# First maximum blocks between half pieces, first keys loaded a chunk sooner, a store wait moved, TensorE's loops written out

## What is computed

```
q = proj(Wq, bq) / math.sqrt(hd);  k = proj(Wk, bk);  v = proj(Wv, bv)
attn = softmax(einsum('bnd,bmd->bnm', q, k), axis=-1)
fuse = einsum('bnm,bmd->bnd', attn, v)
hybrid = conv1x1(concat([x, fuse]), Wf, bf);  x = hybrid * m + x * (1 - m)
# then: depthwise 3x3, gate, 1x1, depthwise 3x3, 1x1, times x
```

## Time and profile before

| what | value |
|---|---|
| median of 3 runs | 4018.02 us (4016.7 to 4024.36) |
| profiled execution, its own time | 4009.41 us |
| its span, first to last instruction | 4007.6 us |
| TensorE busy | 3786.8 us, 94% |
| projection ends, first exponential starts | 281.2 us |
| last exponential starts | 3531.6 us |

### The profile page before, as it was taken

The page is one execution under the profiler, slowest core; times in us unless marked ns, Lnnn a source line. Parts: engine busy times, 40 slices in busy tenths (PEclk is TensorE's granted clock), DMA queues, the critical chain, the costliest instruction groups (busy, mean ns, idle before and its releaser), DMA issues. The chain is left out here.

```text
span 4007.6 us, 74947 instructions
## 1 busy us (share of the span) xinstructions
PE 3786.8 (94%) x19317; PEld 2028.8 (51%) x19317; DVE 3046.2 (76%) x5030; ACT 2923.2 (73%) x5512; POOL 2958.6 (74%) x1359
## 2 busy tenths in 40 slices
PE   7879999999999999999999999999999999959797
PEld 4445555555555555555555555555555555424343
DVE  3357888877877877888777878887778887528989
ACT  1238888888878888888888888888888888812212
POOL 3337888888888888888888888888889888930000
PEclk9989999999999999999999999999999999979898
DMA  6942212221112112212221122112221111122121
GB/s 205 275 126 41 43 22 23 44 43 22 23 27 43 32 22 32 43 32 22 32 43 32 22 33 43 32 22 33 43 32 22 23 22 22 12 76 61 41 64 42
DMA packets 297551, 187.66 MB, mean 47 GB/s; under 512 B 199170, under 2 KB 223924, under 8 KB 297156
## 3 DMA queue, kind: packets, MB, share of 16 engines
q1 hardware_dynamic: 297348, 185.18, 23.8%
HBM read 123.28 MB, written 61.47 MB: 46 GB/s over the span
## 5 line engine op out<-in xcount | busy, mean ns | idle before, releaser
L848 DVE TENSOR_REDUCE block_max<-mx 128x1 f32<-128x512 f32 (+1 forms) x3584 | 2520.5, 759 | 661.0 <-PE mx L619 641.4
L763 ACT ACTIVATE prob<-st 128x512 f32<-128x512 f32 x4096 | 2109.7, 616 | 385.5 <-PE st L608 359.9
L394 POOL TENSOR_TENSOR prob_sum<-prob_sum,prob 128x1024 f32<-128x1024 f32 x768 | 1826.5, 2394 | 26.0 <-POOL prob_sum L394 17.0
L608 PE MATMUL st<-queries,keys 97*128 97x512 f32 x4096 | 1593.6, 409 | 60.6 <-ACT prob L763 36.2
L619 PE MATMUL mx<-keys,max_queries 96*128 96x512 f32 x4096 | 1566.4, 407 | 35.2 <-issue 18.4
L394 POOL TENSOR_TENSOR prob_sum<-prob 128x1024 f32<-128x1024 f32 x384 | 915.9, 2385 | 360.9 <-PE acc L651 345.4
L608 PEld LDWEIGHTS st<-queries,keys 97*128 97x128 f32 x4096 | 772.1, 190 | 539.1 <-issue 236.0
L619 PEld LDWEIGHTS mx<-keys,max_queries 96*128 96x128 f32 x4096 | 777.9, 190 | 431.1 <-ACT tail_exp L753 167.0
L631 PE MATMUL acc<-prob,values 128*32 128x512 f32 x8192 | 993.5, 603 | 0.0
L753 ACT ACTIVATE tail_exp<-mx,negated_max 128x1024 f32<-128x1024 f32 x512 | 575.2, 1123 | 115.5 <-DVE negated_max L852 83.4
L631 PEld LDWEIGHTS acc<-prob,values 128*32 128x32 f32 x8192 | 215.2, 109 | 495.1 <-ACT prob L763 283.0
(11 more groups left out here) (102 smaller groups left out, 1207.5 us busy)
## 6 DMA issues: line engine op xcount, KB each, us to landing
max_queries<-q_scratch SPq DMA_DIRECT2D x384, 64.0 KB
queries<-q_scratch SPq DMA_DIRECT2D x384, 64.0 KB
keys<-k_scratch SPq DMA_DIRECT2D x168, 128.0 KB, 4.8
q_scratch<-keys SPq DMA_DIRECT2D x64, 256.0 KB, 4.8
k_scratch<-keys SPq DMA_DIRECT2D x32, 512.0 KB, 5.1
prob<-in_x SPq DMA_DIRECT2D x16, 512.0 KB, 4.0
v_scratch<-prob SPq DMA_DIRECT2D x16, 512.0 KB, 5.3
queries<-negated_max SPq DMA_DIRECT2D x512, 0.5 KB, 2.0
```

The costliest lines, as they stand in the source:

```text
L394: nc.gpsimd.tensor_tensor(psum[k][:, :, :], a, prob[:, (first + i) % RING, :, :], ALU.add).then_inc(added, 1)
L608: nc.tensor.matmul(st[bank(i, p)][:, :], kk[gp][0:SPLIT + 1, h, s * P:(s + 1) * P], qq[p][:, h, :], start=True, stop=True).then_inc(scores, 1)
L763: nc.scalar.activation(prob[:, s % RING, h, :], st[bank(i, p)][:, :], ACT.Exp).then_inc(exp_done, 1)
L848: nc.vector.tensor_reduce(bmax[p][:, hn, k:k + 1], banks.rearrange("p b n -> p (b n)"), AX.X, ALU.max, negate=True).then_inc(mx_taken, 1)
```

## The change

Five things. `blocks_at` now gives out blocks behind each half of a piece: TensorE issues half a piece (one matmul of q or k, two of v), then one or two blocks. VectorE reduces the blocks of a piece's first half and only then takes the piece before (`take_piece`). SyncE loads the first keys, values and queries after the stores of chunk 8, not 9. ScalarE's wait for the last stores moves from ahead of unit 0 to its exponentials 16 and 28. TensorE's loops over units are written out, with constants in its waits. The sums and products are the same.

```diff
-def blocks_at(n, i):
+def blocks_at(n, i, half):
...
-    slots = BLOCK_CHUNKS * len(PIECES)
-    at = (n - PLAIN_CHUNKS) * len(PIECES) + i
+    slots = BLOCK_CHUNKS * len(PIECES) * 2
+    at = ((n - PLAIN_CHUNKS) * len(PIECES) + i) * 2 + half
     return range(FIRST_BLOCKS * at // slots, FIRST_BLOCKS * (at + 1) // slots)
...
-                if n == PLAIN_CHUNKS - 2:
+                if n == PLAIN_CHUNKS - 3:
...
-            def project(n, p, i):
+            def project(n, p, i, half):
...
-                    for kt in range(CT):
-                        mm = nc.tensor.matmul(pq[k % 2][:, :], w[:, kt, j * P:(j + 1) * P], x[p][:, kt, :],
-                                              start=(kt == 0), stop=(kt == CT - 1))
-                    mm.then_inc(qk_ready, 1)
+                    mm = nc.tensor.matmul(pq[k % 2][:, :], w[:, half, j * P:(j + 1) * P], x[p][:, half, :],
+                                          start=(half == 0), stop=(half == 1))
+                    if half == 1:
+                        mm.then_inc(qk_ready, 1)
...
-            with pe.Fori(0, PAIRS // 2 - 1) as g2:
-                pair(g2, 0, True)
-                pair(g2, 1, True)
-            pair(PAIRS // 2 - 1, 0, True)
-            pair(PAIRS // 2 - 1, 1, False)
+            for u in range(UNITS):
+                unit(u, u % 2, u // NCH % 2, keys_and_queries(u + 1), keys_and_queries(u + 2))
...
+                    if not prev and i == RING:
+                        act.wait_ge(low_ready, 4 * (STEPS + 2))
+                    if not prev and i == 2 * RING - 4:
+                        for q in range(2):
+                            act.wait_ge(v_stored[q], 16 * (1 + STEPS // 2))
...
-            act.wait_ge(low_ready, 4 * (STEPS + 2))
-            for p in range(2):
-                act.wait_ge(v_stored[p], 16 * (1 + STEPS // 2))
...
-                for i, piece in enumerate(PIECES):
-                    if piece[0] == "v":
-                        take_values(n, n % 2, int(piece[1]))
-                    else:
-                        split_projected(n, n % 2, 2 * "qk".index(piece[0]) + int(piece[1]))
-                    for j in blocks_at(n, i):
+                for i, half in itertools.product(range(len(PIECES)), range(2)):
+                    for j in blocks_at(n, i, half):
                         maxima(j // MAXMM, j // MAXMM, older=False, blocks=(j % MAXMM,))
+                    if half == 0 and n * len(PIECES) + i > 0:
+                        take_piece(n * len(PIECES) + i - 1)
+            take_piece(STEPS * len(PIECES) - 1)
```

More of the change, by code:

```diff
@@ L1 @@
+import itertools
 from contextlib import ExitStack
@@ L576, in _ @@
             pe.sem_inc(sums_done, SUMS)
-            def project(n, p, i):
+            def project(n, p, i, half):
                 piece, j = PIECES[i][0], int(PIECES[i][1])
-                if i == 0:
+                if i == 0 and half == 0:
                     pe.wait_ge(x_loaded[p], 16 * (n // 2) + 16)
                 if piece == "v":
-                    pe.wait_ge(v_copied, 2 * n + j + 1)
-                    for s in range(2):
-                        m = 2 * j + s
-                        for kt in range(CT):
[L588 to L593, removed]
+                    if half == 0:
+                        pe.wait_ge(v_copied, 2 * n + j + 1)
+                    m = 2 * j + half
+                    for kt in range(CT):
+                        mm = nc.tensor.matmul(pv[j][:, half, :], x[p][:, kt, m * P:(m + 1) * P], keep["wv"][:, kt, :],
+                                              start=(half == 0 and kt == 0), stop=(kt == CT - 1),
+                                              skip_group_check=True)
+                    if half == 1:
+                        mm.then_inc(v_ready, 1)
+                        if j == 1:
+                            pe.drain().then_inc(x_used, 1)
                 else:
@@ L596, in project @@
                     w = keep["wq" if piece == "q" else "wk"]
-                    pe.wait_ge(full_ready, 4 * n + k + 3)
-                    for kt in range(CT):
-                        mm = nc.tensor.matmul(pq[k % 2][:, :], w[:, kt, j * P:(j + 1) * P], x[p][:, kt, :],
-                                              start=(kt == 0), stop=(kt == CT - 1))
-                    mm.then_inc(qk_ready, 1)
+                    if half == 0:
+                        pe.wait_ge(full_ready, 4 * n + k + 3)
+                    mm = nc.tensor.matmul(pq[k % 2][:, :], w[:, half, j * P:(j + 1) * P], x[p][:, half, :],
+                                          start=(half == 0), stop=(half == 1))
+                    if half == 1:
+                        mm.then_inc(qk_ready, 1)
             def score(u, p, gp, i):
@@ L680, in unit, with keys_and_queries @@
                         max_block(u + 2, p, after[0], n - MAXMM)
[L682 to L693, removed]
+            def keys_and_queries(w):
+                if w >= UNITS:
+                    return None
+                g, c = divmod(w, NCH)
+                return g % 2, Q_INC * (w // 2 + 1), KV_INC * (g // 2 + 1) if c == 0 else None
             for n in range(STEPS):
-                for i in range(len(PIECES)):
-                    project(n, n % 2, i)
-                    for j in blocks_at(n, i):
+                for i, half in itertools.product(range(len(PIECES)), range(2)):
+                    project(n, n % 2, i, half)
+                    for j in blocks_at(n, i, half):
                         if j == 0:
@@ L788, in _ @@
                         take_projected(n, n % 2, 2 * "qk".index(piece[0]) + int(piece[1]))
-                    for j in blocks_at(n, i):
+                    for j in (*blocks_at(n, i, 0), *blocks_at(n, i, 1)):
                         if j % MB == MB - 1:
@@ L822, in take_values, with take_piece @@
                 ins.then_inc(v_copied, 1)
+            def take_piece(at):
+                n, i = divmod(at, len(PIECES))
+                piece, j = PIECES[i][0], int(PIECES[i][1])
+                if piece == "v":
+                    take_values(n, n % 2, j)
+                else:
+                    split_projected(n, n % 2, 2 * "qk".index(piece) + j)
             def invert(v):
```

## The result

The changed kernel took 3965.13 us in the median of six runs (3962.3 to 3982.95), the kernel before 4017.4 (4015.49 to 4024.36) beside it: 52 us less. The ratio over all runs is 0.9878 (95% interval 0.9855 to 0.99); that of the two medians would be 0.987. The forecast was 29.4 us less. The direction is right; the time lies 3.9 us under the low end of the range. The profiled execution's span fell by 47.1 us, from 4007.6 to 3960.5.

| stage | before | after | difference | forecast |
|---|---|---|---|---|
| TensorE goes on in chunk 11 | 167.92 | 167.81 | −0.1 | +1.7 |
| last maximum block starts | 268.9 | 254.8 | −14.1 | −4.5 |
| first exponential starts | 281.2 | 258.2 | −23.0 | −13.1 |
| first to last exponential | 3250.4 | 3225.7 | −24.7 | −16.3 |
| from there to the end | 476.0 | 476.7 | +0.7 | 0 |

What follows compares the result with a forecast made beforehand. TensorE, busy 94% of the span, was taken as the bound, so gains come from its waits or stage ends. Stages ahead 14.1 plus loops 15.3 gave 29.4 us: 4018.0 to 3988.6 us, range 3969 to 4005.

Steps and rivals of the forecast that it cites:

- First keys: At chunk 11, TensorE's 11.1 us wait for keys becomes 14.7 us for the input: 3.5 us lost, bounds 2 to 6.
- The estimate from the rate in the same page's specifications: Loads ahead of chunk 11's input: at 27 GiB/s per DMA engine, 4.6 MB pass in 10 us, input in time.
- Half pieces: Blocks ahead of attention: 5 us from shorter tail waits plus 3 us of clock, 8 us saved, bounds nothing to 12.
- half pieces save nothing: Rival, blocks ahead of attention: VectorE is full and the clock stays low, 8 us less gain; chance 0.18.
- ScalarE's wait: Before attention: first exponential starts once tail and score are there, at 268.1 not 281.19; the moved waits cost nothing.
- Loops written out: Attention: removed outer jumps 7.6 us, clock behind them 5, inner jumps 2.7; sum 15.3 us, bounds 8 and 20.
- The register work behind the waits costs nothing: Attention loops: a block follows a score in 0.23 us there too, so constants in waits were given no gain.
- the clock's 5 us behind outer jumps: Attention: granted clock 0.66 for 5 us and 0.72 for 12 after the outer jumps; 5 us to be won.
- The step on instruction pages: Attention: straight code fetches some 90 more instruction pages, costed at nothing.
- the rival of late pages: Attention: instruction pages held back by the busy DMA queue stop TensorE; at 0.5 us each 4033 us; chance 0.04.
- The likeliest case: Whole kernel: the forecast itself, 3980 to 3996 us; chance 0.55.
- constants in the waits speed up every unit: Rival, attention: half of 0.8 us idle per unit comes back over 60 units, 25 us, giving 3964; chance 0.08.

Runs made afterwards that it cites:

- input_first: The changed kernel with chunk 11's input issued ahead of the first keys; ratio 0.9909 to the kernel before.
- split_loads: input_first with only the first head's keys and six query rows loaded early, the rest behind chunk 10's stores; 3940.01 us, ratio 0.985 to the kernel before.
- halves_only: The kernel before with blocks behind half pieces and VectorE's new order; keys, ScalarE's wait and loops as before; ratio 0.9977.
- inner_out: The changed kernel with TensorE's outer loop back and inner loops written out, so units 1 to 47 wait on registers; 3988.89 us, ratio 0.9973 to the kernel before.
- outer_only: The kernel before with only TensorE's outer loop written out, inner loops and register waits kept; ratio 1.003.
- after_again: The changed kernel run again unchanged, on the chip of the third group; 3954.65 us, ratio 0.99 to the kernel before.
- loops_only: The kernel before with TensorE's loops over units written out and nothing else; ratio 0.9923.

## Why the prediction was right and wrong

**First keys: right, with the loss put 1.8 us too high.** The wait for keys became a wait for chunk 11's input, at the place and with the releaser forecast. The input took 18.3 us to land where 18.9 was assumed, but it was issued at 149.45 instead of 151, and TensorE was back at 167.81 instead of 169.6 (168.6 and 169.35 in two other profiles). With a piece less done that is a loss of 1.7 us where 3.5 was forecast, just under the lower bound of 2. input_first and split_loads show the cause to be the order of the queue: put ahead of the loads, the same input is in time. The Trainium skill's rule on the ring order (DMA: Bandwidth & Descriptors, section Queues, rings and completion order) agrees with this. The estimate from the rate in the same page's specifications does not: by it the input would have come in time, while the DMA engines moved 284 GB/s from 154.6 to 167.8 us with their share at 1.02.

**Half pieces: the mechanism right, the term mis-sized, 8 forecast and 15.8 measured** (14.1 us of the last block and 1.7 of the pause), over its upper bound of 12. Two terms were too small. The waits for the tail fell by 9.4 us, not 5: I had VectorE's start no better than 0.5 us after block 7, and left the pair 0.7 to 1.0 us of wait; the mean is 0.6. And the lost clock came back whole: the 10.2 us at the lower level in this stretch (three dips, two of them in the windows of the earlier trace rows) are gone, about 5.1 us of work, of which I had taken half without a row for it. At the start of the stretch, behind the pause, the clock was low for 3.2 us instead of 6.5, an estimated 1.6 us more. That is 16.1, against 15.8 measured. The rival "half pieces save nothing" is refuted by halves_only. (The forecast's 269.3 for the last block is TensorE's first score; the last block starts at 268.9.)

**ScalarE's wait: right.** From the last block to the first exponential it was 12.3 us before, 3.4 now, 8.9 saved, and 8.6 was forecast (269.3 to 281.2 against 264.8 to 268.1). No moved wait stops ScalarE. That it is also what lets half pieces count in full was not said: without it, halves_only lost 5 us.

**Loops written out: the step that failed is "The register work behind the waits costs nothing".** The term stood at 0 in a sum of 15.3 with 20 as its upper bound, and the attention gave 24.7. Of these the jumps explain 7.6 + 2.7, the low clock (46.8 us before, 41.0 after) half of 5.8, 2.9; some 11.5 are left, 0.2 us a unit, and I had given this mechanism to a rival at 0.08. My evidence was the even 0.23 us from a score to a block, where the work is hidden behind a matmul that runs (no row shows it; the timeline before has score, block, score at 3000.66, 3000.89 and 3001.12). It was not looked for where several waits stand together, at the sums, and there the step is 0.14 us shorter now, and 0.05 at the next unit's first score: 0.19 in a unit, 12 us in 62. inner_out keeps registers without inner jumps and keeps the long step. What was forecast as the clock's 5 us behind outer jumps was not won as such: by the low clock it is 2.9, and outer_only, without those jumps, gained nothing. The step on instruction pages was right in the cost: 150 packets instead of 99 in the instruction queue, 51 more and not 90, and no gap in the attention for them; the rival of late pages is dead.

So of 47.1 us in the profile, the forecast's 29.4 lacked about 8 in the half pieces, 2 in the pause and 8.4 in the attention, less 0.7 lost behind it. The likeliest case and one rival, "constants in the waits speed up every unit", came true together, the rival at half its size; I had treated them as alternatives. That the time fell outside the range is in part chance: 47.1 us taken from 4018 gives 3970.9, just inside it. The profiled execution before lay 8.0 us under its median and the one after 2.8 under its own, which makes the medians' difference 5.2 us larger than the profiles'.

**Open.** The cause of the longer step is shown at the sums; at the next unit's first score it is only argued. inner_out's attention is 47 us longer than after_again's in the profiles (its profiled execution is the slowest of its twelve, after_again's the fastest of its five; the medians lie 34 apart). Its jumps account for 6.8, 0.2 us a unit over 47 units for 9.4, half of its excess of low clock (68.3 against 46.6 us) for 10.9; some 20 us are not explained, and what its 30 more instruction packets cost was not tried. loops_only gained 33 us in the attention and the changed kernel 24.7, so single profiles of the same TensorE code differ by some 8 us. Why the low clock in the attention varies from 37 to 128 us between kernels was not found.

## What to carry to other kernels

A load that is moved ahead in a full queue must be priced with everything that it now stands in front of; to gain, split it and let the small urgent transfer and the stores go first. When matmuls of one kind wait for a chain over two other engines, alternate short runs of them with other work, and let the engine in the middle of the chain do its other work after, not before, what the chain needs; count the clock that the waits cost as part of the gain. That a hidden place costs nothing says nothing of an exposed one: look at register work where several waits meet, and when two mechanisms can both hold, add them up in the range.

## What the runs showed of the hardware

An outer jump back of TensorE cost 3.4 to 3.9 us in four places of two kernels, and 51 more packets of instructions in straight code left no gap in the attention. A wait whose value stands in a register cost nothing visible between back-to-back matmuls (0.23 us from one to the next with either form), and about 0.2 us in a unit of 50 us where waits meet: there the register instructions stand between the last block and the next weight load, 0.47 us from block to sum against 0.33. The chips of the three groups differ by 1.7% in the kernel before (4000.22 to 4068.55 us), more than the whole change; only ratios from one chip could be used.
